# Attention heads of a four-block layer: plain row maximum on VectorE, head factor and row-sum scaling on ScalarE, new order tables

## Chip, cores and metric

One core of one Trainium2 chip. The metric is the device time of one execution in microseconds (us). The kernel before takes 882.39 us (median of 3 runs, 881.47 to 882.75).

## What is computed

Four sub-layers, each `x = x + layernorm(f(layernorm(x)))`, on 1024 tokens of 256 features. The change lies in the first:

```python
def _L0_attn_ref(x, w_qkv, w_out):          # 16 heads of 128, sequence 1024
    qkv = (x @ w_qkv.T).reshape(B, S, 3 * H, D)
    q, k, v = qkv[:, :, :H], qkv[:, :, H:2 * H], qkv[:, :, 2 * H:]
    logits = jnp.einsum('bqhd,bkhd->bhqk', q, k) * scale
    weights = jax.nn.softmax(logits, axis=-1)
    combined = jnp.einsum('bhqk,bkhd->bqhd', weights, v).reshape(B, S, H * D)
    return combined @ w_out.T
```

The others are a feed-forward block with ternary weights ("ffn0"), a latent attention of 16 heads with a causal mask ("latent") and a feed-forward block whose weights are looked up in a table of 16 values ("ffn1").

## The kernel before

One program, five engine queues, each strictly in order, with semaphores between them. Four lists of steps fix the order of work on all queues: `HEADS` comes from a function, `order_of_heads`, and `FFN0`, `LATENT` and `FFN1` are written out as tables of short words. Each engine walks the same list and issues its own part of each step.

**Precision.** Every large product is done as three products of a high and a low half, so each tensor that comes out of PSUM is read twice: ScalarE writes the high half, VectorE the rest (`x` minus high half).

**Heads stage.** There are 32 units; a unit is one head and one half of the query rows (512 rows), in 4 tiles of 128 rows by 1024 keys. A tile of scores fills two PSUM banks, and three such pairs rotate. A tile's steps, in the letters of `order_of_heads`:

- `S` scores on TensorE (6 products of 512 columns);
- `M` row maximum on VectorE (L1674). It is a fused operation: scores plus a tile of zeros, times the head's factor `UNIT(h)` (one value per partition, negative, made on GpSimd), written back over the scores, and the minimum over the row into `nmax`;
- `e` exponential on ScalarE (L1435): `exp(-scores + nmax)` in place, row sum into `rsum`;
- `i` on VectorE: `rsc = rsum / 2^15` (L1682), then `rinv = 1 / rsc` (L1684). The second waits for the first;
- `h` ScalarE writes the high half of the weights `EP` (L1445), and `l` VectorE the rest (L1689);
- SyncE transposes `EP` into `ET` by DMA, and `A` steps on TensorE multiply by the values.

Beside these each unit has three projections for later heads (`X` on TensorE, `x` high half on ScalarE, `y` rest on VectorE), a finish of the unit before (`f` on ScalarE, L1454, `F` on VectorE, L1750), an output projection (`O`, with `o` on VectorE, L1702), weight preparation `w`, and slots `p0` to `p4` which take look-up work for the last block (L1786, L1790) until it is used up. The order of one unit, with the tiles that a step is about as digits, is

```python
    order = ("i3 f0 F0 h3 A7 M0 l3 S0 p0 e0 X0 x0 i0 h0 M1 e1 S1 x1 O0 y0 l0 S2 X1 o0 i1 p1 w1 y1 w0 h1 S3 M2 "
             "p4 A0 A1 X2 A2 A3 l1 p2 e2 x2 i2 A4 M3 A5 A6 h2 y2 l2 w2 p3 e3").split()
```

So VectorE's queue in a unit reads `i3 F0 M0 l3 p0 i0 M1 y0 l0 o0 i1 p1 w1 y1 M2 p4 l1 p2 i2 M3 y2 l2 w2 p3`, ScalarE's `f0 h3 e0 x0 h0 e1 x1 h1 e2 x2 h2 e3`, and TensorE's `A7 S0 X0 S1 O0 S2 X1 S3 A0 A1 X2 A2 ... A6`. The list for the heads is the same after the change.

**The factor.** GpSimd makes `q_unit` in `scale_wqk` from powers of two of the weight norms; it waits until the maxima of the head four before are done, since it overwrites their factor.

Of the kernel before, what the change touches and what calls it, by code (L numbers as in the profile page):

```python
# [238 lines left out]

def order_of_latent():
    return steps_from("""
        d02 s2042 l10 o25 o24 d03 @latent s2062 s2142 l00 p010 o26 o27 p000 s2162 i24 p110 m120 m100 p100 m030 m110
        z2 i25 i26 m020 m010 i27 t21 m130 m000 !latent m220 m200 m320 l11 m230 m210 m310 l01 m300 p011 m330 p001
        p101 p111 A f00 m140 m050 v1 m370 m170 m060 v5 v7 m240 m141 m150 m070 m260 m171 m040 m051 v4 v3 m041 m371
        m160 m061 p210 m151 v0 m161 m071 m250 p211 v2 f01 m261 m360 p200 p201 v6 w00 m340 m520 m241 m270 w01 m350
        m410 m251 w10 f10 m271 p310 m341 m351 w11 m361 m500 m430 f11 w02 m540 m550 w20 m400 m440 w30 m541 m570 w21
        p300 m460 w31 c00 w12 m530 w13 m470 w03 m571 w22 m450 w32 m560 m510 p301 m441 m420 p311 m600 c01 m551 m700
        m740 m750 m730 w04 m561 c02 w23 m451 w33 m471 w14 m720 m610 m630 w34 m461 c03 m760 w24 w05 m751 w15 f20 w06
        m640 m710 w35 f21 p400 c04 w16 m670 w25 m660 w07 p410 m650 y00 m620 p401 w17 m761 w36 c05 w26 m770 m661 p411  # L250
        w27 m771 m671 m820 m840 w37 c06 w40 f30 m910 m641 w50 m741 c07 m651 m920 w41 m800 m810 f31 w51 m830 m940 w60
        m930 w70 m950 m850 m841 m900 p510 p501 p500 w52 w71 c10 m851 w61 ma40 m941 w62 m870 m960 w72 p511 ma30 m860
        c11 ma10 w63 w53 m861 w42 f40 y01 m970 w73 mb20 m971 c12 m951 w43 m961 mb00 ma00 m871 w74 c13 mb10 w44 ma20
        y10 w64 mb40 w45 w75 f41 w54 mb50 w55 w56 ma70 mb30 mb41 w65 ma41 c14 w66 f50 w76 ma50 ma60 p600 w46 p610
        mb60 ma61 c15 w67 ma71 w77 w47 mb70 mb51 p601 ma51 w57 p611 mc20 c16 w90 md00 mb71 mb61 c17 md10 mc30 w80
        f51 w91 md50 w81 mc60 md20 wb0 y11 wa0 md40 mc40 wb1 md70 mc41 mc61 p710 md30 p700 p701 md51 wa1 mc10 c20
        md41 w82 mc50 w83 md71 wa2 md60 mc70 w92 mf40 mc51 c21 mc00 mf10 wb2 w93 me40 w94 md61 p711 me00 mf50 mc71
        mf20 me50 c22 mf00 wa3 f60 wb3 me20 wb4 mf30 me10 wa4 me51 w84 f61 c23 mf41 w95 w85 wa5 mf51 mf70 wb5 me41
        y20 mf60 w96 c24 w86 me60 wa6 me70 c25 wa7 me61 wb6 w87 me71 me30 wb7 mf61 w97 c26 Wc00 mf71 Wd10 f70 c27
        Wc10 f71 Wd00 Wd20 We20 G0 Wf10 We00 Wf30 We10 Wf00 Wd01 Wc01 We01 Wd30 y21 G2 G1 N1 Wf20 C00 Wc11 Wc20 Wc30  # L260
        We30 Wd11 C10 Wf01 C20 C30 Wf31 Wc21 Wf11 y30 We11 Wd41 s3004 We21 Wd31 Wf21 C01 Wc31 G3 Wd21 o31 o33 o30
        C11 o32 We41 Wd51 We61 We31 s3104 N4 Wc41 Wf41 We51 Wd71 Wf51 C21 Wc61 C31 Wc71 i31 i32 Wd61 i30 i33 N0 C41
        Wc51 N5 Wf61 We71 t30 Wf71 C51 C61 S1 C71 N2 N3 u100 y31 u110 @ffn1 s3042 s3062 !ffn1
    """)
# [1936 lines left out]
```

## Time and profile before

| | |
|---|---|
| median of 3 runs | 882.39 us (881.47 to 882.75) |
| the profiled execution | 882.52 us |
| its span | 880.7 us (1.8 us lie around it) |
| heads stage | about 20 to 575 us; M0 of the first unit at 24.6, of the last at 554.3 |
| ffn0, latent, ffn1 | about 575 to 880 us |

One execution is profiled. Busy time is the sum of an engine's instructions. An instruction's row gives its start and its length; the next one of the same engine can start some 0.08 us before the row ends, and for TensorE much earlier (its rows of 0.38 us start every 0.216 us), so a busy share of TensorE says less than that of the others.
### The profile page before, as it was taken

How to read it: one execution, taken by the hardware profiler on the slowest of the kernel's cores; microseconds unless marked ns; L12 is line 12 of the kernel's file. 1: busy time of each engine (PE TensorE's matmuls, PEld its weight loads, DVE VectorE, ACT ScalarE, POOL GpSimd, SP SyncE). 2: the span in 40 equal slices, each digit the busy share in tenths (PEclk: the TensorE clock that was granted, in tenths of full speed). 3: DMA queues.
4: the chain of work that ended last, by engine and by line, in shares of the span. 5: the costliest groups of instructions: out<-in, count | busy, mean ns of one | idle time of the engine just before them, and what ended most of it. 6: DMA issues, size and time to landing. Idle time of an engine off the chain costs nothing.

```text
span 880.7 us, 13310 instructions
## 1 busy us (share of the span) xinstructions
PE 815.8 (93%) x4386; PEld 474.4 (54%) x4386; DVE 770.5 (87%) x1726; ACT 604.2 (69%) x1044; POOL 430.1 (49%) x459
## 2 busy tenths in 40 slices
PE   7889989999999989998998999989988999998997
PEld 3445544455455445454445454567755566564687
DVE  4888999999999999999999999856789898986646
ACT  5777767776778676776766776765765777768632
POOL 3334454444454448678769776125333454544300
PEclk8999999999999999999999999999989999999999
DMA  3588859957788668776875676821000000000001
GB/s 105 123 180 157 151 113 173 194 113 153 166 166 155 127 130 151 148 143 117 161 149 111 124 142 130 155 79 46 1 1 1 1 1 1 1 1 2 1 1 49
DMA packets 276869, 86.32 MB, mean 98 GB/s; under 512 B 267584, under 2 KB 272448, under 8 KB 276416
## 3 DMA queue, kind: packets, MB, share of 16 engines
q1 hardware_dynamic: 275520, 80.05, 47.0%
q0 software_dynamic: 992, 5.34, 2.2%
q8 instruction: 35, 0.57, 0.3%
q14 instruction: 34, 0.28, 0.1%
q10 hardware_dynamic: 288, 0.07, 0.0%
HBM read 17.29 MB, written 1.05 MB: 21 GB/s over the span
## 4 chain that ended last, share of the span: by engine, by line
DVE 41%; PE 38%; issue 9%; ACT 6%; DMA 3%; POOL 2%; DVEq 0%; SPq 0%; ACTq 0%; POOLq 0%
DVE EP L1689 11%; DVE ps L1674 10%; PE ps L1012 6%; PE ps L1014 5%; PE ps L1013 5%; PE ps L1035 4%; DVE ptm L1790 4%; PE ps L1246 3%; PE ps L1050 3%; PE ps L1281 3%; PE ps L1267 3%; DMA ET<-EP 2%; DVE OL L1750 2%; DVE ps L1873 2%; DVE rinv L1684 1%
## 5 line engine op out<-in xcount | busy, mean ns | idle before, releaser
L1445 ACT ACTIVATE EP<-ps,rinv 128x1024 f16<-128x1024 f32 x128 | 142.5, 1113 | 47.5 <-DVE rinv L1684 45.4
L1435 ACT ACTIVATE ps<-ps,nmax 128x1024 f32<-128x1024 f32 x128 | 139.3, 1088 | 49.2 <-DVE nmax L1674 42.8
L1674 DVE CUSTOM_DVE_ANT_0 ps<-ps,zero,q_unit 128x1024 f32<-128x1024 f32 x128 | 163.6, 1278 | 1.6 <-PE ps L1014 1.6
L1689 DVE SCALAR_TENSOR_TENSOR EP<-ps,rinv,EP 128x1024 f16<-128x1024 f32 x128 | 163.4, 1277 | 0.8 <-ACT EP L1445 0.5
L2039 POOL TENSOR_TENSOR wgu<-wgu,ptm 128x688 f32<-128x688 f32 x60 | 99.1, 1651 | 45.3 <-DVE ptm L1790 43.4
L1012 PE MATMUL ps<-ET,VH 128*128 128x512 f16 x256 | 97.0, 379 | 9.5 <-DMA ET<-EP 5.0
L1012 PE MATMUL ps<-K,Q 128*128 128x512 f16 x256 | 97.5, 381 | 8.7 <-DVE KR L1654 4.5
L2039 POOL TENSOR_TENSOR wdn<-wdn,ptm 128x512 f32<-128x512 f32 x45 | 57.2, 1272 | 93.2 <-DVE ptm L1790 92.1
L1014 PE MATMUL ps<-K,QR 128*128 128x512 f16 x256 | 97.0, 379 | 0.0
L1013 PE MATMUL ps<-KR,Q 128*128 128x512 f16 x256 | 97.0, 379 | 0.0
L1014 PE MATMUL ps<-ET,VL 128*128 128x512 f16 x256 | 97.0, 379 | 0.0
L1013 PE MATMUL ps<-ET,VH 128*128 128x512 f16 x256 | 97.0, 379 | 0.0
L1543 ACT ACTIVATE ET<-ps 128x512 f32<-128x512 f32 (+3 forms) x144 | 61.1, 504 | 24.1 <-PE ps L1267 23.2
L1873 DVE CUSTOM_DVE_ANT_0 ps<-ps,tern 128x512 f32<-128x512 f32 (+3 forms) x128 | 72.0, 601 | 4.3 <-PE ps L1246 4.1
L1939 POOL TENSOR_TENSOR rs<-ve,mhalf 128x4 f32<-128x4 f32 (+2 forms) x22 | 19.3, 876 | 100.9 <-DVE ve L1592 80.0
L1012 PE MATMUL ps<-xh,wqh 128*128 128x512 f16 x128 | 49.1, 384 | 9.1 <-DVE KR L1654 6.3
L2101 POOL TENSOR_SCALAR_AFFINE_SELECT ET<-ET 128x128 f32<-128x128 f32 x96 | 28.2, 294 | 44.9 <-ACT ET L1543 38.6
L1012 PEld LDWEIGHTS ps<-ET,VH 128*128 128x128 f16 x256 | 25.7, 100 | 43.4 <-DMA ET<-EP 7.9
L1014 PE MATMUL ps<-xh,wql 128*128 128x512 f16 x128 | 49.0, 383 | 0.0
L1013 PE MATMUL ps<-xl,wqh 128*128 128x512 f16 x128 | 49.0, 383 | 0.0
L1012 PEld LDWEIGHTS ps<-K,Q 128*128 128x128 f16 x256 | 25.0, 98 | 40.7 <-DVE EP L1689 10.4
L1012 PE MATMUL ps<-wvh,xh 128*128 128x256 f16 x128 | 35.0, 273 | 8.4 <-DVE QR L1654 7.0
(256 smaller groups left out, 2119.3 us busy)
## 6 DMA issues: line engine op xcount, KB each, us to landing
wqr<-in_wqk SPq DMA_DIRECT2D x16, 256.0 KB, 3.6
wgu<-in_tern POOLq DMA_DIRECT2D x3, 1024.0 KB, 6.6
wvr<-in_wv SPq DMA_DIRECT2D x8, 256.0 KB, 4.1
wor<-in_wo SPq DMA_DIRECT2D x16, 128.0 KB, 3.1
ET<-EP SPq DMA_TRANSPOSE x128, 4.3
X<-in_x SPq DMA_DIRECT2D x2, 512.0 KB, 5.7
prw<-in_down_idx POOLq DMA_DIRECT2D x2, 256.0 KB, 5.1
tern<-in_l_wuq_rep SPq DMA_DIRECT2D x1, 512.0 KB, 4.1
```

The lines of the kernel that those rows point to most:

```text
L1012: e.matmul(dst, lh, rh, start=first, stop=False)
L1013: e.matmul(dst, lh, rl, start=False, stop=False)
L1014: return e.matmul(dst, ll, rh, start=False, stop=last)
L1035: mm = e.matmul(ps[:, 2 * r + o, :], l, m, start=i == 0, stop=i == len(pairs) - 1)
L1435: e.activation(bank, bank, ACT.Exp, bias=nmax[:, c:c + 1], scale=-1.0, accum_out=rsum[:, c:c + 1]).then_inc(exped.sem, 1)
L1445: e.mul(EP[:, n % NE_RING, 0, :], SB(u, j), rinv[:, c:c + 1]).then_inc(e_hi.sem, 1)
L1543: e.activation(ET[:, r, c:c + n1], ps[:, BANK[(*step, c)][0], n - n1:n], ACT.Exp).then_inc(weight_exped.sem, 1)
L1674: e.tensor_tensor_reduce(SB(u, j), SB(u, j), zero[:, :].broadcast_to([P, 1024]), UNIT(h), 3.0e38, ALU.add, ALU.min, nmax[:, c:c + 1]).then ...
L1689: e.scalar_tensor_tensor(out=EP[:, n % NE_RING, 1, :], in0=SB(u, j), scalar=rinv[:, c:c + 1], in1=EP[:, n % NE_RING, 0, :], op0=ALU.mult, ...
L1790: e.tensor_scalar(ptm[:, v % 2, 0:n], index_tile(t), float(v), lut[:, v:v + 1], ALU.is_equal, ALU.mult).then_inc(picked.sem, 1)
L1873: e.tensor_tensor_reduce(src, src, mask[:, m0:m0 + n], 1.0, -3.0e38 if part == 0 else half, ALU.add, ALU.max, NM[:, p % 2, i8, col:col + 1 ...
L2039: e.tensor_tensor(dst, dst, ptm[:, v % 2, 0:n], ALU.add).then_inc(lut_added.sem, 1)
```

## The change

- `M` becomes a plain maximum of the raw scores, negated, into a new tile `nraw`; the scores stay as they are. The tile of zeros goes, with its fill on GpSimd.
- `e` becomes three ScalarE instructions: `nmax = nraw * UNIT(h)`, the exponential with `scale=UNIT(h)` (a value per partition, where it was the constant -1), and `rsc = rsum / 2^15`. The second waits for the first, the third for the second.
- `i` on VectorE is the reciprocal alone, and waits for ScalarE's `rsc`.
- The factor's sign is turned, and GpSimd's overwriting of it waits for the exponentials of the head four before.
- The tables for ffn0, latent and ffn1 are replaced by others with the same steps in another order.

```diff
 def order_of_ffn0():
     return steps_from("""
-        s1044 V M h000 u020 h010 h020 x000 o14 o15 u030 x010 o17 o16 s1144 u040 h030 h040 x020 x030 u060 x040 i14
+        s1044 V M h000 u020 u030 h010 h020 x000 o16 o17 o14 x010 o15 u040 s1144 h030 u050 h040 x020 h050 x040 i17
...
 def order_of_latent():
     return steps_from("""
-        d02 s2042 l10 o25 o24 d03 @latent s2062 s2142 l00 p010 o26 o27 p000 s2162 i24 p110 m120 m100 p100 m030 m110
+        d02 s2042 l10 o24 o25 d03 @latent s2142 s2062 p010 i24 l00 o26 o27 s2162 p000 p100 i25 p110 m100 z2 m120 i26
...
 def order_of_ffn1():
     return steps_from("""
-        h100 h110 u130 o35 o36 o37 o34 s3142 s3162 u120 x100 h130 i35 x110 i34 i36 i37 u140 t31 h120 h140 u150 x130
+        h110 h100 u120 o34 o35 o37 s3142 o36 s3162 i34 x100 u130 h120 i36 i35 i37 u140 x120 h130 t31 x130 u150 x110
...
@@ scalar engine, "exp"
                     bank = SB(u, j)
-                    e.activation(bank, bank, ACT.Exp, bias=nmax[:, c:c + 1], scale=-1.0,
+                    h = unit(u)[0]
+                    w.wait_ge(*q_back[h])
+                    e.mul(nmax[:, c:c + 1], nraw[:, c:c + 1], UNIT(h)).then_inc(shifted.sem, 1)
+                    w.wait_ge(*shifted[u, j])
+                    e.activation(bank, bank, ACT.Exp, bias=nmax[:, c:c + 1], scale=UNIT(h),
                                  accum_out=rsum[:, c:c + 1]).then_inc(exped.sem, 1)
+                    w.wait_ge(*exped[u, j])
+                    e.mul(rsc[:, c:c + 1], rsum[:, c:c + 1], 1.0 / E_UP).then_inc(sum_down.sem, 1)
@@ vector engine, "max" and "row_inv"
-                    h = unit(u)[0]
-                    w.wait_ge(*q_back[h])
-                    w.wait_ge(*filler_set[1])
-                    e.tensor_tensor_reduce(SB(u, j), SB(u, j), zero[:, :].broadcast_to([P, 1024]), UNIT(h), 3.0e38,
-                                           ALU.add, ALU.min, nmax[:, c:c + 1]).then_inc(maxed.sem, 1)
+                    e.tensor_reduce(nraw[:, c:c + 1], SB(u, j), AX.X, ALU.max,
+                                    negate=True).then_inc(maxed.sem, 1)
                 elif what == "row_inv":
                     u, j = at
                     c = 4 * (u % 2) + j
-                    w.wait_ge(*exped[u, j])
+                    w.wait_ge(*sum_down[u, j])
                     if u >= 2:
                         w.wait_ge(*e_lo[u - 2, j])
-                    e.tensor_scalar(rsc[:, c:c + 1], rsum[:, c:c + 1], 1.0 / E_UP, None, ALU.mult).then_inc(sum_down.sem, 1)
-                    w.wait_ge(*sum_down[u, j])
                     e.reciprocal(rinv[:, c:c + 1], rsc[:, c:c + 1]).then_inc(inverted.sem, 1)
@@ GpSimd
-            e.memset(zero[:, :], 0.0).then_inc(filler_set.sem, 1)
...
-                            w.wait_ge(*maxed[unit_of(h, 1), 3])
+                            w.wait_ge(*exped[unit_of(h, 1), 3])
...
-                    e.tensor_scalar(q_part[:, i0 // 2:i1 // 2], wpow[:, i0:i1:2], -SCALE0 * 2.0 ** 106, None,
+                    e.tensor_scalar(q_part[:, i0 // 2:i1 // 2], wpow[:, i0:i1:2], SCALE0 * 2.0 ** 106, None,
```

## Rows read from the trace of the kernel before

**Rows 1.** The page's head and part 1: busy us, share of span, instructions.

```profile
span 880.7 us, 13310 instructions
PE 815.8 (93%) x4386; PEld 474.4 (54%) x4386; DVE 770.5 (87%) x1726; ACT 604.2 (69%) x1044; POOL 430.1 (49%) x459
```

**Rows 2.** Part 4, the chain that ended last, by line.

```profile
DVE EP L1689 11%; DVE ps L1674 10%; PE ps L1012 6%; PE ps L1014 5%; PE ps L1013 5%; PE ps L1035 4%; DVE ptm L1790 4%; PE ps L1246 3%; PE ps L1050 3%; PE ps L1281 3%; PE ps L1267 3%; DMA ET<-EP 2%; DVE OL L1750 2%; DVE ps L1873 2%; DVE rinv L1684 1%
```

**Rows 3.** Busy time in three stretches: PE, PEld, DVE, ACT, POOL, then PE's clock.

```profile
300.00:560.00 260.00, 241.25 (x1268) 126.88 (x1269) 253.94 (x453) 182.40 (x280) 180.97 (x119) 1.00 0.73 137
100.00:300.00 200.00, 190.00 (x1010) 101.41 (x1008) 190.42 (x371) 148.41 (x243) 95.31 (x81) 1.00 0.79 152
575.00:880.00 305.00, 284.13 (x1619) 196.27 (x1617) 234.49 (x703) 190.08 (x385) 115.66 (x211) 0.98 0.04 12
```

**Rows 4.** VectorE's groups by form: busy us, mean ns, idle before.

```profile
L1674 DVE CUSTOM_DVE_ANT_0 ps<-ps,zero,q_unit 128x1024 f32<-128x1024 f32 x128 | 163.6, 1278 | 1.6 <-PE ps L1014 1.6
L1750 DVE SCALAR_TENSOR_TENSOR OL<-ps,vinv,OH 128x512 fp32r<-128x512 f32 x32 | 23.8, 742 | 7.7 <-ACT OH L1454 7.5
L1663 DVE SCALAR_TENSOR_TENSOR VL<-ps,VH 128x512 f16<-128x512 f32 x32 | 22.0, 686 | 1.8 <-ACT VH L1427 1.6
L1682 DVE TENSOR_SCALAR rsc<-rsum 128x1 f32<-128x1 f32 x128 | 18.7, 146 | 2.8 <-ACT ps L1435 0.8
```

**Rows 5.** ScalarE's groups by form, same columns.

```profile
L1435 ACT ACTIVATE ps<-ps,nmax 128x1024 f32<-128x1024 f32 x128 | 139.3, 1088 | 49.2 <-DVE nmax L1674 42.8
L1454 ACT ACTIVATE OH<-ps,vinv 128x512 fp32r<-128x512 f32 x32 | 21.9, 685 | 19.3 <-PE ps L1014 19.1
L1427 ACT ACTIVATE VH<-ps 128x512 f16<-128x512 f32 x32 | 19.1, 595 | 15.9 <-PE ps L1014 15.7
L1373 ACT ACTIVATE tsc<-ident 128x1 f32<-128x1 f32 x2 | 0.4, 203 | 0.0
```

**Rows 6.** VectorE's timeline in one unit: start, length (us), instruction.

```profile
349.57 1.28 DVE L1674 CUSTOM_DVE_ANT_0 ps<-ps,zero,q_unit 128x1024 f32<-128x1024 f32 x1
...
352.19 0.15 DVE L1682 TENSOR_SCALAR rsc<-rsum 128x1 f32<-128x1 f32 x1
...
352.45 1.27 DVE L1674 CUSTOM_DVE_ANT_0 ps<-ps,zero,q_unit 128x1024 f32<-128x1024 f32 x1
...
362.33 1.27 DVE L1674 CUSTOM_DVE_ANT_0 ps<-ps,zero,q_unit 128x1024 f32<-128x1024 f32 x1
...
365.32 0.14 DVE L1682 TENSOR_SCALAR rsc<-rsum 128x1 f32<-128x1 f32 x1
...
365.57 0.73 DVE L1750 SCALAR_TENSOR_TENSOR OL<-ps,vinv,OH 128x512 fp32r<-128x512 f32 x1
366.22 1.28 DVE L1674 CUSTOM_DVE_ANT_0 ps<-ps,zero,q_unit 128x1024 f32<-128x1024 f32 x1
```

**Rows 7.** ScalarE's timeline in the same unit.

```profile
350.95 1.09 ACT L1435 ACTIVATE ps<-ps,nmax 128x1024 f32<-128x1024 f32 x1 [0.79 <-DVE nmax L1674]
351.96 0.19 ACT L1435 ACTIVATION_READ_ACCUMULATOR ps<-ps,nmax 128x1 f32 x1
352.06 0.59 ACT L1420 ACTIVATE K<-ps 128x512 f16<-128x512 f32 x1
...
364.71 0.19 ACT L1435 ACTIVATION_READ_ACCUMULATOR ps<-ps,nmax 128x1 f32 x1
364.80 0.68 ACT L1454 ACTIVATE OH<-ps,vinv 128x512 fp32r<-128x512 f32 x1
```

**Rows 8.** Who waited for whom, 100 to 300 us: total, times, longest.

```profile
ACT OH L1454 <- PE ps L1014: 8.2, 9, 1.5
```

**Rows 9.** The same, 300 to 560 us.

```profile
PE ps L1012 <- DVE KR L1654: 6.6, 10, 1.4
```

More of the change, by code:

```diff
@@ L233, in order_of_ffn0 @@
     return steps_from("""
-        s1044 V M h000 u020 h010 h020 x000 o14 o15 u030 x010 o17 o16 s1144 u040 h030 h040 x020 x030 u060 x040 i14
-        u050 h060 i15 h050 i17 i16 B u070 h070 t11 x070 D x050 x060 K0 d00 d01 Q u011 s2004 h011 u001 h001 o20 u021
-        x001 z3 h021 x011 K1 o23 o21 o22 u031 s2104 h031 x021 F u041 h041 x031 i22 u051 h051 u061 x041 i21 i20 x051
-        i23 t20 h061 u071 z0 h071 x061 z1 x071 @ffn0 !ffn0
+        s1044 V M h000 u020 u030 h010 h020 x000 o16 o17 o14 x010 o15 u040 s1144 h030 u050 h040 x020 h050 x040 i17
+        x030 i14 i16 u060 i15 B u070 h070 h060 t11 x060 Q x050 x070 K0 s2004 d00 d01 u011 h011 u001 o20 u031 u021
+        h001 x011 o21 o22 o23 D s2104 h021 h031 K1 u041 x021 i21 x001 h041 i22 z3 F u051 x031 i20 i23 u061 x041 h051
+        h061 x051 t20 u071 h071 x061 z0 z1 x071 @ffn0 !ffn0
     """)
@@ L242, in order_of_latent @@
     return steps_from("""
-        d02 s2042 l10 o25 o24 d03 @latent s2062 s2142 l00 p010 o26 o27 p000 s2162 i24 p110 m120 m100 p100 m030 m110
[L244 to L262, printed above, removed]
@@ L263, in order_of_latent @@
-        Wc51 N5 Wf61 We71 t30 Wf71 C51 C61 S1 C71 N2 N3 u100 y31 u110 @ffn1 s3042 s3062 !ffn1
+        d02 s2042 l10 o24 o25 d03 @latent s2142 s2062 p010 i24 l00 o26 o27 s2162 p000 p100 i25 p110 m100 z2 m120 i26
+        m110 m020 i27 m030 m010 t21 m000 m130 !latent m320 m310 m220 m330 l11 m200 m210 m230 l01 m300 p011 p001 p101
+        p111 A m170 m160 v4 m070 v3 m340 f00 m370 v7 m260 m040 m050 m060 m150 v5 p210 m041 p211 m240 m140 m161 m051
+        m151 m171 v0 m061 m141 m071 v1 m360 m250 v6 m261 f01 m361 p200 v2 p201 m270 w10 m540 m410 m341 m520 w00 m350
@@ new lines, in order_of_latent @@
+        w11 m271 w01 m351 m251 m500 m241 m371 p310 w02 f10 m430 f11 p300 w12 m530 w20 m440 w30 m420 m550 w21 m470
+        m570 w31 m541 m571 m441 c00 w22 m400 m730 w13 m510 m700 p311 m720 m560 p301 m450 w03 m561 c01 m551 w04 m460
+        w14 m600 w32 m750 m461 w23 m471 m670 c02 m740 w05 m451 w33 m660 m760 w15 m661 m640 c03 m761 w24 f20 m751 w34
+        f21 w35 p400 w25 m610 p401 m630 c04 w06 w16 p410 y00 m650 w26 w36 w07 m770 w17 m651 m620 c05 m800 w27 m840
+        m820 p411 m710 w37 m771 m910 c06 m641 w50 m671 w40 m841 m741 p510 m810 f30 m920 c07 w51 m850 f31 w41 m930
@@ new lines, in order_of_latent @@
+        m830 w70 m940 m900 p501 w71 w60 p500 m851 w61 p511 m970 c10 m950 w62 w72 m870 ma40 m960 m860 c11 w63 mb20
+        w52 m941 m971 w53 f40 w54 ma00 ma20 w73 w42 y01 w43 m951 ma30 m961 m861 w44 ma10 mb10 c12 m871 w45 ma70 mb40
+        c13 ma41 mb00 w74 w64 mb50 f41 w55 mb30 c14 w65 w75 mb41 w76 w46 mb60 f50 w56 w57 ma60 w66 y10 ma61 p600
+        p610 w47 mb70 c15 w77 ma50 ma71 mb71 p601 w67 p611 c16 mc30 w90 mb61 ma51 md00 c17 mb51 w91 mc20 md20 w80
+        f51 w81 mc60 md10 wb0 mc10 y11 wa0 md70 wb1 md50 md30 md40 p710 mc50 mc40 p700 p701 mc51 md51 c20 w82 mc70
@@ new lines, in order_of_latent @@
+        w92 mf00 mc61 wa1 mc41 wa2 mc71 mc00 p711 mf40 me00 md71 md41 md60 c21 w83 mf10 wb2 mf70 me40 me50 md61 w93
+        c22 wa3 me51 mf30 wb3 f60 wa4 mf50 w84 me10 w94 w85 mf60 c23 mf51 w86 w95 mf41 me30 wa5 wb4 me70 wb5 f61
+        me41 mf20 c24 w87 w96 me60 mf61 me20 c25 wa6 w97 y20 wb6 wa7 wb7 me71 mf71 c26 Wc00 me61 c27 Wd00 f70 Wc10
+        f71 Wd20 Wd30 Wc20 N1 G1 We30 We10 We00 Wc30 Wf00 Wd10 y21 Wf30 We01 Wc01 Wf10 C00 Wf20 Wc11 G2 We20 We21
+        Wf01 Wc31 C10 C20 C30 Wd31 Wf11 G0 Wf31 y30 Wf21 Wd01 s3004 Wd11 We11 Wd41 Wc21 We41 o32 o31 o30 o33 C01
@@ L264, in order_of_latent @@
+        Wd21 C11 Wf41 Wd51 We31 s3104 C21 Wc41 N0 Wc61 Wf51 G3 Wc71 Wf61 C31 Wd61 We51 Wc51 C41 i32 i30 i31 i33 We61
+        We71 Wd71 N4 N2 t30 Wf71 C51 S1 N5 C61 N3 C71 u100 y31 u110 @ffn1 s3042 s3062 !ffn1
     """)
@@ L268, in order_of_ffn1 @@
     return steps_from("""
-        h100 h110 u130 o35 o36 o37 o34 s3142 s3162 u120 x100 h130 i35 x110 i34 i36 i37 u140 t31 h120 h140 u150 x130
-        u101 u111 h150 d10 x140 d11 u121 x120 h101 u131 x150 h111 s4004 o40 h121 u141 u151 x101 o41 o42 x111 x121
-        h131 o43 d12 x131 h141 d13 x141 h151 x151 s4042 o44 s4061 o45 s4071 o46 o47
+        h110 h100 u120 o34 o35 o37 s3142 o36 s3162 i34 x100 u130 h120 i36 i35 i37 u140 x120 h130 t31 x130 u150 x110
+        u121 d10 d11 h150 h140 x140 x150 s4004 u101 h101 u111 h121 u131 u141 h111 o40 x111 x101 u151 d12 x121 h141
+        o41 o42 h131 x141 h151 x131 d13 x151 o43 s4042 o44 s4061 o45 o46 s4071 o47
     """)
@@ L315, in build @@
         filler = sbuf(top, "filler", [P, 512], BF16)
-        zero = sbuf(top, "zero", [P, 1])
         with ExitStack() as ctx:
@@ L338, in build @@
             nmax = sbuf(ctx, "nmax", [P, 8])
+            nraw = sbuf(ctx, "nraw", [P, 8])
             rsum = sbuf(ctx, "rsum", [P, 8])
@@ L447, in build @@
         qkv_lo, maxed, e_lo, o_lo, inverted = (signal(n, "DVE") for n in ("qkv_lo", "maxed", "e_lo", "o_lo", "inverted"))
-        o_added, sum_down = signal("o_added", "DVE"), signal("sum_down", "DVE")
+        shifted = signal("shifted", "ACT")
+        o_added, sum_down = signal("o_added", "DVE"), signal("sum_down", "ACT")
         abs_summed, all_summed = signal("abs_summed", "ACT"), signal("all_summed", "PE")
@@ L562, in build @@
         filler_set.mark(0)
-        filler_set.mark(1)
         ones_in.mark(0)
@@ L606, in build @@
             elif what == "exp":
+                shifted.mark(*at)
                 exped.mark(*at)
+                sum_down.mark(*at)
             elif what == "row_inv":
-                sum_down.mark(*at)
                 inverted.mark(*at)
```

## The prediction

> **What bounds the kernel now.** I read the page's shares first: TensorE 93% busy, VectorE 87%, ScalarE 69% [rows 1]. A share over the whole span mixes stages, so the chain of work that ended last comes next: its two dearest lines are VectorE's, L1689 and the row maximum L1674 [rows 2], both of the heads stage. Then the busy time by stretch: from 300 to 560 us VectorE works 253.9 of 260 us (98%) and ScalarE 182.4 (70%); from 100 to 300 VectorE has 190.4 of 200 (95%) and TensorE looks just as full, 190.0; after 575 us VectorE has 234.5 of 305 [rows 3]. So the late half of the heads is VectorE's. The early half is shared: ScalarE's finish L1454 waits there for TensorE's last product of the unit before, 9 times for 8.2 us [rows 8], and VectorE's finish waits for that. What VectorE saves in front of such a point is worth nothing.
>
> **What VectorE saves.** The small scaling L1682 goes: 128 of them, 146 ns each [rows 4]. In the queue it costs more than its row, from its start to that of the reciprocal 0.17 to 0.18 us. I take 0.17. The maximum: today 1278 ns with a pointer operand (`q_unit`) [rows 4]. Rows of 512 columns from PSUM take 742 ns with a pointer and 686 without, so a pointer costs 56; from 512 to 1024 columns is 1278 - 742 = 536 ns. A maximum without pointer is then 686 + 536 = 1222 ns, 0.06 us less. That is the likely value; no large tensor_reduce is in the trace. Bounds: 0 saved (same pipeline), and 0.14 saved, if what writes its result out as a row of its own today also held the queue. Together 0.23 us a tile, 0.92 a unit, 29.4 us over 128 tiles. In the 15 units that VectorE governs (M0 from 295.6 to 540 us) it is 13.8.
>
> The Trainium skill ("VectorE: DVE Perf Modes", rules for kernel authors) speaks against such a step: tensor_reduce on a hot path is called the slowest VectorE operation, and only its 1x form exists. The trace has the fused operation at 1278 ns too, also one element per cycle, so the rule would make the term 0 at worst here; no row shows a large tensor_reduce.
>
> **What ScalarE pays.** Three additions per tile. The exponential gets a second pointer operand: 685 ns with one against 595 without [rows 5], +0.09 us. The multiplication by `UNIT(h)` has one value per partition: the only such row is 203 ns [rows 5]; with the pointer's 0.09 I take 0.28 (bounds 0.20 and 0.30). The row-sum scaling 0.19 (bounds 0.15 and 0.20). Each hands over by semaphore, about 0.04 us: L1682 starts at 352.19, the accumulator row ends at 351.96 + 0.19 = 352.15 [rows 6, 7].
>
> The Trainium skill ("ScalarE: Activation LUTs", rules for kernel authors) says to put multiplications on VectorE and not ScalarE. By size that is fair: 146 ns on VectorE against about 0.2 us. But the queue that pays is another one, and which of them governs decides, so the rule alone gives no time.
>
> Now the chain of a tile, from the start of its maximum to that of its `i` on VectorE. Before: 352.19 - 349.57 = 2.62 us [rows 6]. After: maximum 1.22, hand-over 0.04, multiplication 0.28, hand-over 0.04, exponential to the end of its accumulator row 1.20 + 0.09 = 1.29 (350.95 to 352.15 before [rows 7]), hand-over, scaling and hand-over 0.27: 3.13 us. So `i` can't start until 0.51 us later (bounds 0.41 and 0.61). The next ScalarE instruction, today 0.09 behind the start of the accumulator row (352.06, 364.80 [rows 7]), starts 0.55 us later after the maximum than now. ScalarE's queue gets some 0.65 us a tile longer, 83 us in all; with 70% busy in the late half it comes to about 88%, and is not itself full.
>
> **What of it is hidden.** For each of the 124 stretches from one maximum to the next I compared, in the timelines, when `i` could have started with when it did. What counts is the slack s: VectorE arrives 0.06 us earlier and the sum comes 0.51 later, so it stalls for 0.57 - s. For the finish F0, if f0 follows the accumulator row directly, the like is 0.78 - s: VectorE gets there 0.23 earlier and f0's end comes 0.55 later. The unit of rows 6 and 7 has both kinds:
> - `i0` at 352.19 has slack 0: a stall of 0.57, so M0 to M1 goes from 2.88 to 3.22;
> - `i1` has 0.96 to 0.98 in 28 of the 31 units: nothing stalls;
> - `i2` here 2.09, since the slots p4 and p2 are filled;
> - F0 at 365.57, with f0 ending at 365.48: slack 0.05, a stall of 0.73 [rows 6, 7].
>
> Over the 15 units from 295.6 us on: `i0` has slack 0 four times and 0.26 seven times: 4 x 0.57 + 7 x 0.31 = 4.5 us. `i2`: 0.26 four times, 0 once: 1.8 us. End of the unit (`i3` or F0): 0.33, three of 0.31, three of 0.73, one of 0.58: 4.0 us. Stalls 10.3 us against 13.8 saved: 3.5 us gained. With the chain 0.10 shorter it is 5.9, with 0.10 longer 1.1. What is late next, where VectorE no longer stalls, is TensorE: 60 products of 512 columns at 0.216 us and 24 of 256 columns at some 0.11 make 15.7 us of a unit's 16 to 18.
>
> **The early half** (16 units). The same count on `i0` (slack 0 or 0.17 in most) makes M0 to M1 0.16 to 0.34 longer, and the M0 that starts it is set by TensorE's last product through f0 and F0. Behind M1 comes `y0`, whose PSUM bank the projection X1 on TensorE waits for; in the late half that pair already costs TensorE 6.6 us in 10 waits [rows 9]. From the end of A7, TensorE has S0, X0, S1, O0 and S2 before X1 (4 x 1.3 + 0.7 = 5.9 us). `y0` is done, from the same point, after f0 and F0 (1.4), M0 to M1 (2.9), the maximum (1.2) and its own 0.7: 6.2 now, 6.5 after. Bounds: -3.5 us (nothing reaches TensorE and VectorE's gain counts at times) and +4 (0.25 us in each of 16). I take +1.0, nearer to nothing, since later steps of the unit give back part. The last two units have no look-up work to fill slots, and their `i0`, `i2` and `i3` have slack 0: beyond what is counted, +0.5.
>
> **Edits without a price.** The fill of `zero` runs on GpSimd before the first weights are there; the changed wait for the factor is on work of the head four before, some 60 us old; the sign is free. No DMA is moved, and SyncE's queue is as before.
>
> **The tables.** Same steps, same engines, same durations. After 575 us TensorE is busy 284.1 of 305 with the clock at 0.98 of full [rows 3]; some 21 us of idle, start and end included, and a short dip of the clock are all that an order can win or lose. I can't say which from the words: 0, bounds -4 and +4.
>
> **Sum.** Profiled execution 882.52 (span 880.7 and 1.8 around it; 0.13 over the median). -3.5 + 1.0 + 0.5 + 0 = -2.0: 880.5 us.
>
> **Rivals.**
> 1. VectorE's time comes through (the small ScalarE operations overlap more than rows let me think, and the stalls don't add): -13.8 in the late half: 868.7; half of that 875. For: VectorE 98% busy. Against: slacks of 0 at `i0` and F0 are in the trace.
> 2. Slower: ScalarE's longer tile goes on to TensorE. Place: `i0` -> M1 -> `y0` -> X1. Price: M0 to M1 0.34 longer in each of 31 units, +10.5 us and nothing of the rest saved, as TensorE's own queue sets the unit: 893; with half the units 888. It decides as soon as TensorE's idle time per unit, about 1.4 us in the early half, is already all waits for VectorE. For: rows 9 and slack 0 at `i0`. Against: in the late half VectorE, not TensorE, is full.
> 3. The maximum is no shorter: 0.06 x 60 = 3.6 us of the gain go and the chain is 0.06 longer (some 1.2 us): 885. This is also what the skill's rule on tensor_reduce would come to here.
> 4. The heads are as I say and the tables make it: 876.5 or 884.5.
>
> **Chances.** Forecast (877 to 884) 0.42; rival 1 0.17; rival 2 0.18; rival 3 0.12; rival 4 0.11. A measurement of this kernel can tell about 0.2% from no change, 1.8 us, so "same" is 880.6 to 884.2. Faster: half of the forecast, rival 1 and part of 4, 0.42. Same: 0.24. Slower: rivals 2, 3 and part of 4, 0.34. The range takes nearly all of rival 1's gain and most of rival 2: 869 to 891.
>
> **What will show it.** Right: the maximum's row at about 1222 ns, one reciprocal per tile without L1682 before it; three ScalarE rows of 0.28, 1.18 and 0.19; M0 to M1 at 3.2 us or above in nearly every unit; VectorE below 95% from 300 to 560, with "idle before" on the reciprocal, released by ScalarE, of some 8 us; heads stage 2 us shorter; the rest of the kernel within 4 us of 305. Wrong: M0 to M1 still at 2.9 (rival 1), waits of TensorE for L1654 well above those of rows 9 (rival 2), a maximum of 1.28 (rival 3), or a heads stage that keeps its length while the end moves (rival 4).

## The result, and the profile after

The kernel after takes 886.58 us (median of 5 runs, 884.89 to 886.67), the one before, beside it, 881.47 (5 runs, 880.71 to 882.75). The ratio on record is 1.0044, interval 1.0029 to 1.0059: slower by 0.44%, where 880.5 us and faster were forecast. The two medians by themselves are 0.58% apart, so the loss is some 4 to 5 us. The profiled execution took 886.67 us, 4.15 more than that of before.

The page's head and part 1, which answer to [rows 1]:

```profile
span 884.8 us, 13432 instructions
PE 817.7 (92%) x4385; PEld 474.2 (54%) x4386; DVE 748.3 (85%) x1470; ACT 666.9 (75%) x1300; POOL 430.7 (49%) x458
```

VectorE has 22.2 us less to do, and the kernel is longer. Busy time by stretch, as [rows 3]:

```profile
300.00:560.00 260.00, 243.62 (x1282) 128.51 (x1281) 244.89 (x336) 213.88 (x403) 183.59 (x120) 1.00 0.74 139
100.00:300.00 200.00, 188.74 (x997) 99.67 (x996) 179.59 (x275) 171.13 (x337) 95.79 (x82) 1.00 0.78 150
575.00:880.00 305.00, 285.22 (x1627) 195.65 (x1626) 238.28 (x711) 192.89 (x392) 114.41 (x210) 0.99 0.04 12
```

From 300 to 560 us VectorE fell from 98% to 94% and TensorE did 2.4 us more: the late half runs faster. From 100 to 300 VectorE fell from 95% to 90% and TensorE did 1.3 us less: there the time saved became waiting, and more. The groups of VectorE and ScalarE by form, as [rows 4] and [rows 5]:

```profile
L1678 DVE TENSOR_REDUCE nraw<-ps 128x1 f32<-128x1024 f32 x128 | 155.4, 1214 | 3.3 <-PE ps L1015 2.7 <-issue 0.5
L1752 DVE SCALAR_TENSOR_TENSOR OL<-ps,vinv,OH 128x512 fp32r<-128x512 f32 x32 | 23.9, 746 | 12.3 <-ACT OH L1461 12.3
L1686 DVE RECIPROCAL rinv<-rsc 128x1 f32<-128x1 f32 x128 | 20.2, 158 | 25.3 <-ACT rsc L1443 24.2
...
L1440 ACT ACTIVATE ps<-ps,nmax,q_unit 128x1024 f32<-128x1024 f32 x128 | 150.7, 1177 | 4.3
L1438 ACT ACTIVATE nmax<-nraw,q_unit 128x1 f32<-128x1 f32 x128 | 37.6, 294 | 38.7 <-DVE nraw L1678 38.6
L1443 ACT ACTIVATE rsc<-rsum 128x1 f32<-128x1 f32 x128 | 26.0, 203 | 4.0
L1440 ACT ACTIVATION_READ_ACCUMULATOR ps<-ps,nmax,q_unit 128x1 f32 x128 | 24.5, 191 | 0.0
L1461 ACT ACTIVATE OH<-ps,vinv 128x512 fp32r<-128x512 f32 x32 | 21.7, 678 | 7.9 <-PE ps L1015 7.7
```

Every size is close to its forecast: the maximum 1214 ns (1222), the multiplication 294 (280), the exponential 1177 (1178), the scaling 203 (190). What is new is the last column. The reciprocal waits 24.2 us for ScalarE, and the finish (L1752) 12.3, from 7.7 [rows 4]. VectorE's timeline in the unit of [rows 6], then ScalarE's, as [rows 7]:

```profile
354.66 0.75 DVE L1752 SCALAR_TENSOR_TENSOR OL<-ps,vinv,OH 128x512 fp32r<-128x512 f32 x1 [0.34 <-ACT OH L1461]
355.33 1.22 DVE L1678 TENSOR_REDUCE nraw<-ps 128x1 f32<-128x1024 f32 x1
356.46 1.28 DVE L1691 SCALAR_TENSOR_TENSOR EP<-ps,rinv,EP 128x1024 f16<-128x1024 f32 x1
358.47 0.16 DVE L1686 RECIPROCAL rinv<-rsc 128x1 f32<-128x1 f32 x1 [0.73 <-ACT rsc L1443]
358.55 1.22 DVE L1678 TENSOR_REDUCE nraw<-ps 128x1 f32<-128x1024 f32 x1
```

```profile
356.58 0.29 ACT L1438 ACTIVATE nmax<-nraw,q_unit 128x1 f32<-128x1 f32 x1 [0.94 <-DVE nraw L1678]
356.91 1.18 ACT L1440 ACTIVATE ps<-ps,nmax,q_unit 128x1024 f32<-128x1024 f32 x1
358.01 0.19 ACT L1440 ACTIVATION_READ_ACCUMULATOR ps<-ps,nmax,q_unit 128x1 f32 x1
358.24 0.20 ACT L1443 ACTIVATE rsc<-rsum 128x1 f32<-128x1 f32 x1
358.35 0.58 ACT L1421 ACTIVATE K<-ps 128x512 f16<-128x512 f32 x1
```

From maximum to `i` it is 358.47 - 355.33 = 3.14 us (forecast 3.13, before 2.62) and from M0 to M1 3.22 (forecast 3.22). In 24 of the first 31 units M0 to M1 is 3.21 to 3.23.

So where is the time? The table cuts the trace at the first maximum M0 of units 0, 4, 16 and 31, at the first scaled activation of ffn0 (`f0si`, L1356 before, L1357 after) and at the end. All numbers are differences of the starts of rows, in us; the last four columns are experiments, below.

| stretch | before | after | tables only | late units only | early units only | units 4 to 31 |
|---|---|---|---|---|---|---|
| start to M0 of unit 0 | 24.6 | 25.7 | 25.8 | 25.4 | 25.5 | 25.1 |
| units 0 to 3 | 65.4 | 68.6 | 65.4 | 65.2 | 68.6 | 65.7 |
| units 4 to 15 | 205.6 | 207.9 | 206.0 | 206.0 | 207.6 | 207.1 |
| units 16 to 30 | 258.7 | 255.7 | 258.7 | 255.7 | 258.7 | 255.6 |
| M0 of unit 31 to `f0si` | 33.4 | 35.6 | 33.4 | 34.3 | 33.4 | 35.8 |
| `f0si` to the end | 293.0 | 291.4 | 292.7 | 292.1 | 292.4 | 292.1 |
| span | 880.7 | 884.8 | 882.0 | 878.6 | 886.1 | 881.4 |

The late half gained 3.0 us. The first 16 units lost 3.2 + 2.3 = 5.5, more than half of it in the first four.

Those four begin like this. After's VectorE in unit 0, and TensorE behind it:

```profile
30.56 0.17 DVE L1686 RECIPROCAL rinv<-rsc 128x1 f32<-128x1 f32 x1 [1.05 <-ACT rsc L1443]
...
34.66 0.16 DVE L1686 RECIPROCAL rinv<-rsc 128x1 f32<-128x1 f32 x1 [0.33 <-ACT rsc L1443]
...
37.41 1.28 DVE L1691 SCALAR_TENSOR_TENSOR EP<-ps,rinv,EP 128x1024 f16<-128x1024 f32 x1 [0.80 <-ACT EP L1452]
38.61 0.68 DVE L1661 SCALAR_TENSOR_TENSOR KR<-ps,K 128x512 f16<-128x512 f32 x1
```

```profile
37.05 0.27 PE L1015 MATMUL ps<-wvh,xl 128*128 128x256 f16 x1
39.34 0.28 PE L1013 MATMUL ps<-wvh,xh 128*128 128x256 f16 x1 [2.02 <-DVE KR L1661]
...
40.84 0.64 PE L1013 MATMUL ps<-K,Q 128*128 128x512 f16 x1
41.27 0.63 PE L1014 MATMUL ps<-KR,Q 128*128 128x512 f16 x1
41.70 0.63 PE L1015 MATMUL ps<-K,QR 128*128 128x512 f16 x1
...
43.41 0.62 PE L1013 MATMUL ps<-xh,wqh 128*128 128x512 f16 x1
43.83 0.41 PE L1014 MATMUL ps<-xl,wqh 128*128 128x512 f16 x1
44.08 0.38 PE L1015 MATMUL ps<-xh,wql 128*128 128x512 f16 x1
```

The same two places where only the tables are new (that trace has the heads of before):

```profile
30.04 0.15 DVE L1682 TENSOR_SCALAR rsc<-rsum 128x1 f32<-128x1 f32 x1 [0.41 <-ACT ps L1435]
...
37.60 0.68 DVE L1654 SCALAR_TENSOR_TENSOR KR<-ps,K 128x512 f16<-128x512 f32 x1
```

```profile
38.33 0.28 PE L1012 MATMUL ps<-wvh,xh 128*128 128x256 f16 x1 [1.34 <-DVE KR L1654]
```

Three waits of VectorE for ScalarE, 1.05, 0.33 and 0.80, put `KR` off by 1.1 us (38.61 - 25.70 from the first maximum, against 37.60 - 25.83); TensorE's idle time, which ends with it, grows from 1.34 to 2.02.
```profile
40.00:46.00 6.00, 5.32 (x31) 2.69 (x29) 5.82 (x11) 5.39 (x8) 1.40 (x2) 1.00 1.06 199
```

```profile
40.00:46.00 6.00, 6.00 (x25) 2.73 (x23) 4.18 (x6) 4.12 (x8) 0.72 (x1) 0.72 1.08 216
```

### The profile page after: what moved, and what is told of

It reads as the page before. It is cut to its first block and busy times, and to the rows that moved or that the text cites. A ratio compares the mean times of both kernels' runs of the same rounds, so it can differ in the third digit from the quotient of the medians.

```text
span 884.8 us, 13432 instructions
## 1 busy us (share of the span) xinstructions
PE 817.7 (92%) x4385; PEld 474.2 (54%) x4386; DVE 748.3 (85%) x1470; ACT 666.9 (75%) x1300; POOL 430.7 (49%) x458
## 3 DMA queue, kind: packets, MB, share of 16 engines
HBM read 17.29 MB, written 1.05 MB: 21 GB/s over the span
## 5 line engine op out<-in xcount | busy, mean ns | idle before, releaser
L1678 DVE TENSOR_REDUCE nraw<-ps 128x1 f32<-128x1024 f32 x128 | 155.4, 1214 | 3.3 <-PE ps L1015 2.7
L1440 ACT ACTIVATE ps<-ps,nmax,q_unit 128x1024 f32<-128x1024 f32 x128 | 150.7, 1177 | 4.3
L1438 ACT ACTIVATE nmax<-nraw,q_unit 128x1 f32<-128x1 f32 x128 | 37.6, 294 | 38.7 <-DVE nraw L1678 38.6
L1013 PEld LDWEIGHTS ps<-ET,VH 128*128 128x128 f16 x256 | 25.8, 101 | 43.7 <-DVE VL L1670 8.2
L1013 PEld LDWEIGHTS ps<-K,Q 128*128 128x128 f16 x256 | 25.1, 98 | 39.3 <-DVE EP L1691 11.3
```

The costliest lines, as they stand in the source:

```text
L1013: e.matmul(dst, lh, rh, start=first, stop=False)
L1438: e.mul(nmax[:, c:c + 1], nraw[:, c:c + 1], UNIT(h)).then_inc(shifted.sem, 1)
L1678: e.tensor_reduce(nraw[:, c:c + 1], SB(u, j), AX.X, ALU.max, negate=True).then_inc(maxed.sem, 1)
```

## The experiments

Each was run 4 times (before_o0) to 12 times beside the kernel before on the same chip; times are medians, and stretches are from the one execution that was profiled. The median of before was 883.7, 883.0 and 882.7 us in the batches; what a kernel is worth is given against it, with the interval of the ratio.

### The heads alone, the tables alone

heads_only is the kernel after with the tables of before; tables_only is before with the new tables.

> The heads part of the change alone, with the old tables for ffn0, latent and ffn1. The changed kernel's trace lies 4.1 us over before: +1.1 at the first row maximum, +2.5 over the first two units, +2.9 over units 2 to 15, -3.0 over units 16 to 30, +2.3 from there to ffn0, -1.7 after. Theory A (the heads part makes all of the loss, the new tables give a little back): 887 to 889, ratio 1.006 to 1.008, and ffn0 to end at 293 us as before. Theory B (the new tables cost, or the loss is a start that happened to be slow): 882 to 884, and the first maximum at 24.6.

> The new tables alone, heads as before. Theory A: 1.5 to 2 us faster than before (880), as ffn0 to end takes 291.3 in place of 293.0. Theory B: 885, slower. If the clock's dips at 645 and 810 us of before decide, not the order, the time is within 1 us of before.

heads_only: 888.62 us, ratio 1.006 (1.0048 to 1.0073), +4.9 us. tables_only: 882.93, ratio 0.9991 (0.9982 to 1.0), -0.8, where 880 was expected. All of the loss is the heads'. The tables' term, 0, was right within its bound. In the heads stage the trace of tables_only repeats that of before (65.4, 258.7, 33.4 in the table; units 4 to 15 differ by 0.4), but starts 1.2 us later. The first M0 is at 25.1 to 26.4 us in all the other traces, with or without the change: the 24.6 of before was a quick start of that execution, not something that the change took away.

### One half of the change at a time

sum_only moves the row-sum scaling to ScalarE and keeps the fused maximum:

```diff
 scalar engine, "exp"
+                    w.wait_ge(*exped[u, j])
+                    e.mul(rsc[:, c:c + 1], rsum[:, c:c + 1], 1.0 / E_UP).then_inc(sum_down.sem, 1)
 vector engine, "row_inv"
-                    e.tensor_scalar(rsc[:, c:c + 1], rsum[:, c:c + 1], 1.0 / E_UP, None, ALU.mult).then_inc(sum_down.sem, 1)
```

max_only has the plain maximum, ScalarE's multiplication and the pointer scale, and keeps the scaling of the row sum on VectorE.

> The row-sum scaling alone goes to ScalarE; maximum and exponential as before, old tables. VectorE is 0.17 us a tile shorter, the way from a maximum to the reciprocal 0.23 longer (2.85 us). Theory A (what counts is the stall at the reciprocal where its slack is below the added time; ScalarE's length by itself costs nothing): most slacks are 0.17 or 0.26, so most of the 0.17 x 128 comes through in the late half: -6 to -8 there, 0 to +1 in the early half: 875 to 878. Theory C (ScalarE's queue is the limit, any instruction on it costs): 882 to 886.

> The other part alone: plain maximum on VectorE, multiplication and pointer scale on ScalarE, old tables; the row-sum scaling stays on VectorE. VectorE is 0.06 us a tile shorter, the way from a maximum to the first of the two small operations 0.29 longer (2.91 us). Theory A: nearly all slacks of 0, 0.17 and 0.26 are eaten, little is saved: +3 to +6, 885 to 888. Theory C: like the sum alone or worse by the ratio of ScalarE's additions (0.42 to 0.24 us a tile), 884 to 888. Both: slower; the two parts' losses tell apart only with the run of the sum.

sum_only: 877.81 us, ratio 0.993 (0.9916 to 0.9944), -5.9. max_only: 885.19, ratio 1.002 (1.001 to 1.0031), +1.5, less than the +3 to +6 expected. So the parts have opposite signs, and they don't add: -5.9 + 1.5 = -4.4, and both together are +4.9. VectorE's `i0` in the same unit as above, in sum_only and in max_only:

```profile
351.27 0.16 DVE L1684 RECIPROCAL rinv<-rsc 128x1 f32<-128x1 f32 x1 [0.44 <-ACT rsc L1438]
```

```profile
354.30 0.15 DVE L1684 TENSOR_SCALAR rsc<-rsum 128x1 f32<-128x1 f32 x1 [0.50 <-ACT ps L1440]
```

Each part alone makes the way from maximum to `i` 2.91 us, 0.3 longer than before; together it is 3.14. In seven of the 15 late units `i0` had 0.26 us of slack, so the first 0.3 is nearly free there and what comes on top of it is all stall. Over the first 300 us `i` waits 6.0 us for ScalarE in sum_only and 7.2 in max_only, and 15.3 in after; VectorE's saving there is 64 x 0.23 = 14.7.

### What VectorE saves against what the chain costs

no_scale leaves the scaling of the row sum out of the computation (no multiplication by 1/2^15 anywhere): `rinv` is the reciprocal of `rsum`, and nothing else changes. chain_delay leaves VectorE's work as it is and puts a copy of the row sum on ScalarE into the chain:

```diff
+                    w.wait_ge(*exped[u, j])
+                    e.mul(rcopy[:, c:c + 1], rsum[:, c:c + 1], 1.0).then_inc(sum_copied.sem, 1)
...
-                    w.wait_ge(*exped[u, j])
+                    w.wait_ge(*sum_copied[u, j])
```

> Before with the scaling of the row sum left out: the reciprocal is taken of the unscaled row sum, so the attention weights are 2^15 too small. This is VectorE's saving of 0.17 us a tile alone, with no ScalarE instruction and a way from maximum to reciprocal that is no longer. The run of the row-sum scaling on ScalarE gave -5.9 us. Theory A (saving minus stalls from a longer way): 128 x 0.17 = 21.8 us are saved, of which TensorE's limits in the early half leave half: -13 to -16, 868 to 871. If ScalarE's extra instruction cost nothing (the early half alone keeps the gain small), this run is no better than -7: 877.

> Before, with one more ScalarE instruction of one column behind each exponential, which copies the row sum; VectorE's scaling reads the copy. VectorE's work is as before, the way from maximum to VectorE's first small operation is 0.23 us longer, and ScalarE's queue 0.3 us a tile longer. Theory A: it costs 0.23 us less the slack wherever the slack is below: +4 to +7, 888 to 891, and together with the run without the scaling it makes the -5.9 us of the moved scaling. Theory C (ScalarE's length counts in every tile): 0.3 x 128 = 38 us of which half shows, above 895.

no_scale: 871.27 us, ratio 0.9865 (0.9843 to 0.9887), -11.7: taking 0.17 us out of each of 128 tiles (21.8 us) brings half of it to the end, a little less than the 13 to 16 expected. chain_delay: 888.65, ratio 1.0066 (1.0048 to 1.0083), +5.7: 0.23 us more in each chain (29.4 us) costs a fifth. The sum, -6.0, agrees with sum_only's -5.9; the intervals leave some 2.5 us either way, so that it agrees to 0.1 is luck. chain_delay makes the chain and ScalarE's queue longer at once, so the two aren't told apart; but that every addition to ScalarE's queue costs its time, which would have given more than 895, is ruled out.

By stretch the two runs show where a saving counts. The profiled executions, against before's 205.6 and 258.7 us (table):

| stretch | VectorE's saving | no_scale | chain_delay |
|---|---|---|---|
| units 4 to 15 | 48 x 0.17 = 8.2 | 204.6 (-1.0) | 208.2 (+2.6) |
| units 16 to 30 | 60 x 0.17 = 10.2 | 250.8 (-7.9) | 261.6 (+2.9) |

Unit 8 of no_scale is 2.6 us longer than before's: TensorE waits there 2.2 us for the DMA that writes `ET`. The other 11 units of that row save 3.5 of 7.5 us. So less than half of VectorE's saving comes through in units 4 to 15, and three quarters in units 16 to 30, while the longer chain costs 0.2 us a unit in both. In units 16 to 30 the two add up to -5.0, and sum_only has -5.2 there (253.5 us).

### Another order of a unit

If M1 or X1 waits because of what stands before them, moving the output projection `O0 o0` to the front should give the heads change room:

```diff
-    order = ("i3 f0 F0 h3 A7 M0 l3 S0 p0 e0 X0 x0 i0 h0 M1 e1 S1 x1 O0 y0 l0 S2 X1 o0 i1 p1 w1 y1 w0 h1 S3 M2 "
+    order = ("i3 f0 F0 h3 A7 M0 l3 S0 O0 p0 e0 X0 x0 o0 i0 h0 M1 e1 S1 x1 y0 l0 S2 X1 i1 p1 w1 y1 w0 h1 S3 M2 "
```

> The heads part of the change with old tables (888.6 us), and two steps moved in the order of a unit: the output projection O0 goes from behind S1 to right behind S0 on TensorE, its addition o0 on VectorE from behind l0 to before i0. VectorE then has 0.6 us of work to do where it now stalls for i0 (3.14 us after the maximum, 2.3 to 2.8 of work before it), and takes it from the next stretch, which has 3.5 us of work against 3.14. X1 on TensorE no longer waits for y0 but for o0, which is earlier. Theory A: 0.3 to 0.5 us a unit are won, 875 to 880. Theory C (ScalarE's queue is full): 887 to 889, unchanged.

> Before, with the same two steps moved and nothing else. The reciprocal at i0 could start 2.62 us after the maximum and VectorE arrives at 2.4 to 2.9, so little stalls there; the stretch after loses slack (0.97 to 0.4) without a stall. Theory A: 0.1 us a unit from i0, and what X1's earlier start brings TensorE (its 12 us of waits for L1654 in all): 878 to 883. If it wins as much as in the changed kernel, the move helps for another reason than the stall at i0.

heads_o0: 898.58 us, ratio 1.0168 (1.0145 to 1.0191). before_o0: 899.14, ratio 1.0181 (1.0161 to 1.02). Both expectations were missed: the order itself costs 16 us. `O0` needs F0's result, which isn't there, and the scores S1 behind it come late: VectorE's maximum waits 12.6 us for TensorE over the heads stage, where it was 1.6 [rows 4]. TensorE's waits from 300 to 560 us in before_o0 have a line that [rows 9]'s view hasn't:

```profile
PE ps L1012 <- DVE OL L1750: 4.0, 6, 0.9
```

With that order the heads change costs nothing that can be told (898.6 against 899.1, from 5 and 4 runs that overlap): M0 to M1, now 4.1 us in many units, waits for TensorE, and the longer chain hides behind it. The same edit is worth +5 or about 0 by what else is late at the same place.

### Late units, early units, all but the first four

`NEW(h)` chooses between the heads of after and of before by the head, in the maximum, the exponential, the reciprocal and the sign of the factor; the tables are those of before, and GpSimd's wait before it overwrites the factor is that of after in all units:

```diff
+        def NEW(h):
+            return h >= 8
```

It is `h >= 8` (units 16 to 31) in late_heads, `h < 8` (units 0 to 15) in early_heads, `h >= 2` (units 4 to 31) in heads_from4.

> The heads change in units 16 to 31 alone; units 0 to 15 and the tables as before. If the change gains in the late half and loses in the early one (theory), this runs about 3 us faster than before, 880 us, with units 16 to 30 some 3 us shorter and the early half as before. If its cost lies in every unit alike (rival), half of what the heads change costs in all (+4.9) is left: 885 to 886.

> The heads change in units 0 to 15 alone. Theory: the loss is here, 4 to 6 us slower than before, 887 to 889, and with the run that has only the late units the sum is that of all units. Rival (the same in every unit): 885 to 886. As forecast ahead of the result (+1.0 in the early half) it would be 884.

> The heads change in all units but the first four (heads 0 and 1 as before). In the traces the first maximum of unit 1 comes 2.3 us later with the change, 1.6 of it behind TensorE's clock, which halves at about 41 us after TensorE waited for VectorE. If that is the change's doing, this run is 2 to 2.6 us faster than the heads change in all units, about 886. If the clock falls there anyhow, or the time is given back, it is within 1 us of it, 888.

late_heads: 881.01 us, ratio 0.9982 (0.9972 to 0.9993), -1.7. early_heads: 888.96, ratio 1.0068 (1.0053 to 1.0083), +6.3. Their sum, +4.6, fits heads_only's +4.9, and in the table late_heads has after's 255.7 us for units 16 to 30, early_heads after's 68.6 for units 0 to 3. The gain is in the late half, the loss in the early one. heads_from4: 884.07, ratio 1.0013 (1.0004 to 1.0023), +1.4. Leaving out the four first of 32 units takes 3.5 us off the +4.9, more than the 2 to 2.6 expected. The clock stays at its full level there, as TensorE's wait is the short one again:

```profile
37.64 0.28 PE L1022 MATMUL ps<-wvh,xh 128*128 128x256 f16 x1 [1.34 <-DVE KR L1672]
...
39.40 0.38 PE L1024 MATMUL ps<-K,QR 128*128 128x512 f16 x1
39.61 0.38 PE L1022 MATMUL ps<-K,Q 128*128 128x512 f16 x1
```

In the trace it shows 65.7 us for the first four units against 68.2 in heads_only. The other 1 us of the 3.5 lies within the intervals of the two runs and has no place.

### The better part with the tables

sum_tables is sum_only with the new tables.

> The row-sum scaling alone on ScalarE, the maximum as before, with the new tables. The parts lie in different stages and should add: -5.9 and -0.8, so 876 to 877 us. If the tables are worth nothing here, 877.8.

875.52 us, ratio 0.9916 (0.9902 to 0.9929): 7.2 us faster than before, and some 11 faster than after (another batch). It is the version to keep. From 300 to 560 us TensorE does more than in after (243.62), and VectorE is at 97%:

```profile
300.00:560.00 260.00, 245.38 (x1294) 129.56 (x1295) 250.95 (x401) 195.80 (x347) 182.81 (x120) 1.00 0.76 139
```

## Why the prediction was wrong, point by point

**Right: the sizes and the chain.** 0.23 us saved a tile, 0.51 added to the chain, M0 to M1 at 3.22. The slack formula (0.57 - s at `i`, with the 0.23 saved) gives +1.4 and +2.0 us for M0 to M1 in units 0 to 3 and 4 to 15; after has +1.5 and +2.1 against tables_only.

**Right: the late half.** -3.5 forecast, -3.0 measured, and the same in late_heads. The stalls of VectorE for ScalarE's `rsc` from 300 to 560 us are 7.0 us, where "some 8 us" was named. ScalarE's busy share there was put at 88%; 0.65 us in each of 60 tiles on top of 182.4 of 260 is 85%, and it measured 82%. Nothing rested on it.

**The failed step: the early half, +1.0.** It was 3.2 + 2.3 = +5.5 against the trace of before and +5.1 against tables_only, above the bound of +4, and it turned the sign of the whole. It holds two errors.
1. *Units 0 to 3, +3.2.* The price was taken as 0.25 us in each unit at most. The place was named (`i0`, M1, `y0`, X1), but the first units weren't read by themselves. `order_of_heads` gives unit 0 a list of steps of its own, not the order printed above, and unit 0 has no work of a unit before it to fill the queues: VectorE waits there for `rsc` and `EP` three times, 2.2 us in all, against once for 0.41. What made this dear is less the wait than TensorE's clock, at its lower level for 3 us: 1.5 of unit 0's 2.4 us. It fell behind this wait in each of the four traces that have the heads change in unit 0 (after, heads_only, early_heads, heads_o0) and in none of the other ten. No term of the sum allowed for the clock. heads_from4 shows the size: the loss against before goes from 4.9 to 1.4 us.
2. *Units 4 to 15, +1.9 to +2.3* (heads_from4 has +1.6 against before and +1.1 against tables_only). "Later steps of the unit give back part" was the reason to take a value nearer to nothing, and it hardly held. The formula would have given these 12 units -3.0 us. The trace has M0 to M1 as computed, but M1 to M2 gives back 1.5 where 2.8 was VectorE's, and M3 to the next M0, where the formula has -2.2, has +1.0. Two things meet there. In six of the 12 units of after f0 waits for TensorE's last product, and what VectorE saves ahead of it is worth nothing. In three others (6, 10 and 14) f0 waits for nothing but ScalarE's own longer queue, and F0 stalls 0.41 us for it. The first is less often the case than before: ScalarE now comes later itself. From 100 to 300 us, where [rows 8] has 8.2 us in 9 waits, after has

```profile
ACT OH L1461 <- PE ps L1015: 3.1, 6, 0.7
```

How the 3.2 us between formula and trace divide between the two isn't shown. That VectorE's saving is cut short there even without a longer chain is: in no_scale 11 of these units get 3.5 of 7.5 us, and the twelfth gets longer, while the late half gets 7.9 of 10.2. The prediction said in its first part that a saving ahead of f0 is worth nothing, and then let it count in part.

Rival 2 named a sign of its own, TensorE's waits for VectorE's `KR`. From before to after they grow, from 20 to 300 us, from 5.6 to 7.3 us, and from 300 to 560 us from 6.6 [rows 9] to

```profile
PE ps L1013 <- DVE KR L1661: 7.6, 10, 1.2
```

So the projections come late by 1.7 us more in the early half, of which 0.7 in unit 0, and by 1.0 in the late one. Rival 2 had the right place and sign there. Its full price, +10.5 in 31 units, is far too large, as the late half gained; its milder form, half of the units at 888 us, is within 1.5 us of the result. That form had 5.3 us for 16 units and the early half paid 5.5; as 1.5 of that is the clock's, which the rival doesn't have, part of the agreement is luck.

**The last two units, +0.5.** 34.3 us in late_heads against 33.4: +0.9. After itself has 35.6; the rest is again the clock, as ffn0 begins: heads_only, whose clock stays up there, has 34.2, and heads_from4, where it falls at 575 us, 35.8. From 575 to 590 us it is 0.89 in after and 1.00 in before, where it dips later. After, then before twice:

```profile
575.00:590.00 15.00, 12.91 (x62) 7.28 (x61) 6.32 (x18) 9.35 (x15) 1.21 (x2) 0.89 0.18 35
```

```profile
575.00:590.00 15.00, 14.35 (x79) 10.20 (x77) 6.14 (x17) 6.82 (x11) 1.16 (x3) 1.00 0.05 12
640.00:660.00 20.00, 16.16 (x68) 11.54 (x66) 17.01 (x59) 12.48 (x22) 7.44 (x10) 0.83 0.00 1
```

A dip less behind `f0si` is the likely reason why the rest of the kernel is 1.7 us shorter in after. Where the dips fall isn't a matter of the order of the tables alone: behind `f0si` the tables of before, late_heads and early_heads are the same, and the granted clock from 590 to 875 us is 0.98, 0.99 and 0.99. The runs of the tables alone put order and dips together at -0.8 us.

**Sum.** Forecast -3.5 + 1.0 + 0.5 + 0 = -2.0. Measured in the profiled executions: -3.0 late, +5.5 early, +2.3 at the end of the heads, -1.7 after, +1.1 at the start = +4.2, of which the start is before's quick run. Rival 1 fell with M0 to M1 at 3.22, rival 3 with the maximum at 1214 ns, rival 4 with heads_only.

**The order of the parts** was not in the prediction at all: it priced the change as a whole, and the moved scaling alone is worth -5.9 us. With the table of slacks at hand, the sum could have been made for each edit: in the late half the first 0.3 us on the chain goes mostly into slack, and the next isn't free.

## What to carry to other kernels

Price each edit of a bundle by itself against the slack on its chain: two edits that each fit can together overrun it, and here -5.9 and +1.5 us became +4.9. Sum by stage, and read the first and last units by themselves; where an engine waits for another one at the end of each unit, a good part of the saving ahead of that wait is lost (in no_scale more than half in units 4 to 15, a quarter in units 16 to 30). And look at every TensorE idle time that the change makes longer: here 0.7 us more of waiting cost another 1.5 us of clock, though an idle time as long elsewhere cost none.

## What the runs showed of the hardware

- TensorE's clock in unit 0 stayed at its upper level after idle times of 1.34 us (before, tables_only, heads_from4) and 1.6 us (sum_only, max_only, chain_delay), and fell to 1.2 GHz, for 3 us, after 2.0 us (after, heads_only, early_heads, heads_o0). The products before and after are the same; only the idle time and what VectorE and ScalarE do differ.
- But the length of the idle time doesn't decide it by itself. In no_scale an idle time of 2.19 us that ends at 168.1 us left the granted clock at 1.00, and at the same place of the same order two kernels differ, before_o0 first:

```profile
201.63 0.39 PE L1012 MATMUL ps<-xh,wqh 128*128 128x512 f16 x1 [2.24 <-DVE XN L1702]
```

```profile
203.87 0.61 PE L1013 MATMUL ps<-xh,wqh 128*128 128x512 f16 x1 [2.16 <-DVE XN L1704]
```

The first goes on at full speed (granted clock 1.00 from 200 to 210 us), the second, after the shorter idle time, at half (0.83). What the chip reacts to isn't shown.

- A plain maximum of 128x1024 from PSUM is 1214 ns, and the fused operation with a pointer operand (a value per partition) 1278: the plain form is not slower. The Trainium skill ("VectorE: DVE Perf Modes", rules for kernel authors) calls tensor_reduce the slowest operation of VectorE; the traces don't bear that out for this shape.
- On ScalarE a pointer for the scale costs the same 0.09 us on one value per partition (294 against 203 ns) as on 1024 (1177 against 1088).
- The time to the first M0 varies from 24.6 to 26.4 us over the 14 profiled executions, with the change in the first units or without it.
